# Cross-attention's first maxima ahead of the other batch's open sums, in VectorE's order of a decoder layer

## The reference

```python
x = x + attention(layernorm(x), Wq, bq, Wk, bk, Wv, bv, Wo)        # two corner scores set to -1e9
# cross-attention: the softmax runs over the heads, not over the keys
Q, K, V = split_heads(query @ Wq + bq), split_heads(ctx @ Wk + bk), split_heads(ctx @ Wv + bv)
energy = jnp.einsum('bhqd,bhkd->bhqk', Q, K) / sqrt(16)
energy = jnp.where(mask == 0, -1e10, energy)
attention = jax.nn.softmax(energy, axis=1)
x = x + jnp.einsum('bhqk,bhkd->bhqd', attention, V) merged @ Wo + bo
x = x + nvfp4_linear(silu(nvfp4_linear(ln(x), gate)) * nvfp4_linear(ln(x), up), down)
```

## Time and profile before

| | us |
|---|---|
| median of 3 runs (lowest, highest) | 573.68 (573.54, 574.16) |
| the profiled execution, its own time | 574.91 |
| its span in the profile | 573.2 |
| TensorE busy | 532.9 (93%) |
| VectorE busy | 503.2 (88%) |
| ScalarE busy | 344.8 (60%) |
| GpSimd busy | 343.8 (60%) |

### The profile page before, as it was taken

The page is one execution under the profiler, slowest core; times in us unless marked ns, Lnnn a source line. Parts: engine busy times, 40 slices in busy tenths (PEclk is TensorE's granted clock), DMA queues, the critical chain, the costliest instruction groups (busy, mean ns, idle before and its releaser), DMA issues. The chain is left out here.

```text
span 573.2 us, 14885 instructions
## 1 busy us (share of the span) xinstructions
PE 532.9 (93%) x6148; PEld 384.5 (67%) x6157; DVE 503.2 (88%) x674; ACT 344.8 (60%) x601; POOL 343.8 (60%) x262
## 2 busy tenths in 40 slices
PE   7899999999899999999999999999999887989787
PEld 6777777777567777777776777777777643534444
DVE  5887888798889888898899899899899989899987
ACT  3655766767554665467565765675568454766644
POOL 3111424323318776777897979867898885666750
PEclk9999999999999999999999999999999988989997
DMA  8910000000110011101110111011100000000001
GB/s 217 314 64 1 2 3 3 2 1 2 42 40 1 11 39 48 48 6 45 48 44 4 50 48 45 6 48 48 39 11 9 9 11 8 1 19 19 20 18 56
DMA packets 16645, 20.78 MB, mean 36 GB/s; under 512 B 2821, under 2 KB 14322, under 8 KB 16578
## 3 DMA queue, kind: packets, MB, share of 16 engines
q1 hardware_dynamic: 14800, 19.18, 11.2%
q10 hardware_dynamic: 1778, 0.66, 0.6%
HBM read 16.16 MB, written 1.84 MB: 31 GB/s over the span
## 5 line engine op out<-in xcount | busy, mean ns | idle before, releaser
L427 POOL TENSOR_TENSOR work<-work,rden 125x1792 f32<-125x1792 f32 x48 | 172.5, 3593 | 3.8
L1029 ACT ACTIVATE work<-scores 125x896 f32<-125x896 f32 x96 | 88.9, 985 | 95.4 <-PE scores L1458 95.4
L717 DVE TENSOR_REDUCE negmax<-scores 125x112 bf16<-125x1792 f32 x48 | 97.2, 2025 | 18.6 <-PE scores L1448 18.1
L725 DVE TENSOR_REDUCE den<-work 125x56 f32<-125x896 f32 x96 | 102.4, 1066 | 10.1 <-ACT work L1029 10.0
L425 POOL TENSOR_TENSOR rden<-rden,stays 125x112 f32<-125x112 f32 x48 | 22.2, 462 | 64.7 <-DVE rden L730 63.9
L1448 PE MATMUL scores<-qz,kT 32*125 32x224 f32 x768 | 50.5, 377 | 2.4 <-ACT work L1029 1.7
L1458 PE MATMUL scores<-negmax,identb 125*125 125x448 bf16 x192 | 45.1, 357 | 7.8 <-DVE negmax L717 7.6
L1484 PE MATMUL head_out<-work,v 125*32 125x112 f32 x1536 | 49.2, 268 | 0.0
L1555 PE MATMUL wide<-ctxT,ck 128*128 128x375 f32 x128 | 48.6, 500 | 0.0
L630 DVE TENSOR_REDUCE a_mpad<-scores 112x8 bf16<-112x896 f32 x32 | 33.5, 1092 | 15.2 <-PE scores L1350 15.1
L1569 PE MATMUL wide<-cv,ctxT 128*125 128x256 f32 x192 | 46.7, 379 | 0.0
(11 more groups left out here) (274 smaller groups left out, 1174.3 us busy)
## 6 DMA issues: line engine op xcount, KB each, us to landing
ctx_sb<-in_ctx SPq DMA_DIRECT2D x16, 375.0 KB
mask_sb<-in_mask_Bx1xSxS_if SPq DMA_DIRECT2D x16, 164.1 KB, 5.6
xsx<-in_x SPq DMA_DIRECT2D x4, 448.0 KB, 10.1
out_x<-ores SPq DMA_DIRECT2D x6, 256.0 KB, 2.2
a_raw_w<-in_L_ffn_gate_w SPq DMA_DIRECT2D x1, 1024.0 KB, 9.0
a_raw_w<-in_L_ffn_up_w SPq DMA_DIRECT2D x1, 1024.0 KB, 11.6
a_raw_w<-in_L_ffn_down_w SPq DMA_DIRECT2D x1, 1024.0 KB, 13.6
xt<-xsx SPq DMA_DIRECT2D x4, 112.0 KB, 2.2
```

Source lines behind the costliest of these rows:

```text
L427: pool.tensor_tensor(ex2[0:KP, kc], ex2[0:KP, kc], over, ALU.mult).then_inc(s["prob"], 1)
L717: dve.tensor_reduce(negmax[0:KP, :], scores[0:KP, :, 0:4 * TOK].rearrange("p j (h t) -> p t j h", h=4), AX.XY, ALU.max, negate=True).then_ ...
L725: link(dve.tensor_reduce(den[0:KP, kc, half], ex2[0:KP, kc, :, half, :].rearrange("p g t s -> p t g s"), AX.XY, ALU.add))
L1029: act.activation(ex2[0:KP, kc, 4 * i:4 * i + 4].rearrange("p (j m) t s -> p j m s t", m=NE), scores[0:KP, 2 * i:2 * i + 2, 0:4 * TOK].rear ...
```

## The change

In VectorE's loop over the turns of cross-attention, the maxima of (now, 0) are issued ahead of the first half sum of (old, 2) instead of behind it. The two instructions and all others stay as they are, and no wait is added or removed. In turn 0 there is no `old` and the order is the same.

```diff
                     third, fourth = early(n, 2), early(n, 3)
+                    if now:
+                        key_max(now, 0)
                     if old:
                         head_sum(old, 2, 0)
-                    if now:
-                        key_max(now, 0)
                     if n == 0:
                         outputs(B - 1)
```

## The result

| | before | after |
|---|---|---|
| median of 14 runs each, us | 573.92 (572.97 to 575.71) | 572.17 (570.44 to 573.13) |
| after / before, 95% interval | | 0.9963 (0.9952 to 0.9975) |
| profiled execution: span, us | 573.2 | 569.4 |
| its granted clock of TensorE, mean | 0.982 | 0.991 |
| start of the first maxima of turn 0 | 157.03 | 157.46 |

The kernel became 0.37% faster (0.25 to 0.48%): 573.92 x 0.0037 = 2.1 us; the two medians themselves are 1.75 us apart. The forecast was 571.9 and 1.8 us. The stretch from the first maxima of turn 0 to those of turn 15 was the same in the two profiled executions of either kernel, to 0.04 us, and most of what follows is read from it.

A forecast was written before the change was run, and what follows sets the result against it. TensorE bounds cross-attention's turns, VectorE counting only where TensorE waits for it. Gained 3.88 less 2.07 given back nets -1.81 us: from the 573.68 median to 571.9, a gain of 0.3%, range 570.4 to 574.0.

The forecast's parts named there:

- the eight latenesses: First maxima of turns 5, 7, 8, 9, 10, 12, 14, 15 start when scores are there: 3.88 us gained.
- turns in time: the second maxima don't move: Turns 2 to 6, 8, 10, 12, 13: idle pieces of 1.07 take up the half sum's 1.06, costing nothing.
- turns 7 and 9: Second maxima late, partly hidden before the exponentials, and third maxima late: 0.18 given back each, 0.36 together.
- turn 11 into 12: x_varp, tied to GpSimd's qz, holds VectorE 0.44 longer, delaying turn 12's first maxima: 0.42 given back, bounds 0.1 and 0.92.
- GpSimd in 6, 8, 10, 13: Product for the last third of keys comes 1.06 later, 1.03 hidden: 0.38 given back in all, bounds nothing and 4.24.
- turn 14: GpSimd's scale chain waits for VectorE's block maxima, 0.21 later, delaying its product and qz: 0.45 given back, bounds 0.18 and 1.06.
- turn 15, second maxima: No idle ahead of them, so 1.06 is paid, less 0.60 from a shorter instruction: 0.46 given back, bounds 0.46 and 1.06.
- 0.14 after the end of the scores is the earliest start: Read from turn 6: first maxima can start no sooner than 0.14 after scores end; lateness is counted from there.
- The late second maxima: In turns 7, 9, 11 and 14, one more instruction leaves 0.62 idle for 1.06: second maxima 0.44 late.
- The slower rival: GpSimd bounds turns 6, 8, 10, 13 if its 1.03 is not slack: 4.24 paid, net +2.05, 575.7 us; chance 0.10.
- The two holds: Instructions held by GpSimd's products shorten: turn 1's tiny one from 1.375 to under 0.5, turn 15's from 1.23 to 0.63.
- a rival for no change: Give-backs double (573.9 us) or TensorE's clock takes the gain, a slow stretch being worth near 1.5 (573.4); chance 0.22.

The follow-up runs named there:

- Run 5: The change made only in the late turns 5, 7, 8, 9, 10, 12, 14 and 15, against the kernel before; ratio 0.9954 (0.9935 to 0.9972).
- run 3: Order of the kernel before, but VectorE doesn't wait for the end of each first half sum, against the kernel before; ratio 0.9974 (0.9960 to 0.9989).
- run 8: The change plus no wait of VectorE for its own first half sums, against the kernel before; ratio 0.9928 (0.9902 to 0.9953).
- run 6: The change in all turns but 7, 9, 11, 14 and 15, against the kernel before; ratio 0.9951 (0.9935 to 0.9967).
- Run 10: The change in all turns but 15, against the kernel before; ratio 0.9942 (0.9923 to 0.9961).
- run 7: The change plus x_shifted moved behind the second maxima in its five turns, against the kernel before; ratio 1.0042 (1.0022 to 1.0062).

## Why the prediction was right

Point by point, in us of the loop, taken from turn lengths (end of the first scores to the next) in the profiles:

| step | forecast | measured |
|---|---|---|
| the eight latenesses gone | 3.88 | 3.88, but for turn 12 (below) |
| start 0.06 instead of 0.14 after the scores, 15 turns | none | 15 x 0.08 = 1.2 |
| turns in time: the second maxima don't move | 0 | 0 (0.13 to 0.14 behind their scores) |
| turns 7 and 9 | -0.36 | -0.28 - 0.27 |
| turn 11 into 12 | -0.42 | -0.22 - 0.27 |
| GpSimd in 6, 8, 10, 13 | -0.38 | about -0.05 |
| turn 14 | -0.45 | -0.54 |
| turn 15, second maxima | -0.46 | -0.53 |
| sum | 1.81 | 2.9; seen as a whole, 302.52 - 299.59 = 2.9 |

For the measured column the turn of before without its lateness and without the 0.08 is the base. Turn 7 was 19.07 - 0.22 - 0.08 = 18.77 long and became 19.05. Turn 14 was 19.14 - 0.23 - 0.08 = 18.83 and became 19.37.

**What bounds the kernel** was read rightly: TensorE sets the turn, and VectorE's lateness is TensorE's to the last tenth. Run 5 shows that the eight turns named by the rows hold the gain.

**The number is nearer than the account.** Forecast 1.8, measured 1.75 by the medians and 2.1 by the ratio: that closeness is in part luck. Up to the third maxima of turn 15 the change is worth 2.9 at an equal clock, 1.1 more than forecast. The medians show less because the changed kernel's executions had the lower clock more often, which no step of the prediction foresaw.

**The step that was mis-sized** is "0.14 after the end of the scores is the earliest start". That was read from turns in which a half sum with its own wait stood ahead of the maxima; run 3 shows that the wait made 0.08 of it. It is worth 1.2 in the change.

**The late second maxima** were 0.52 late in turns 7, 9 and 11, not 0.44, and the third ones of 7 and 9 0.21. The 0.44 was 1.06 - 0.62. From the first to the second maxima of turn 7 VectorE took 298.39 - 291.46 = 6.93 where it had taken 298.58 - 292.19 = 6.39, so 0.54 more: in its new place the half sum takes 1.12 up to the next instruction (293.40 to 294.52), and not 1.06, and the last half sum takes 1.11 up to the maxima (297.28 to 298.39), where the one before took 1.08 up to its idle time. In turn 15 it is 0.53 for the 0.46. Without VectorE's waits for its first half sums (run 8) the 6.93 is 6.68, so these waits have a share in it; which of the 0.10 is theirs no run shows.

**GpSimd** was late by 1.06 as worked out, and its product ended at the very moment at which TensorE wants it, but the 0.05 of a handover that I had put on top was already within the slack: 0.38 became 0.05. The slower rival rested on this place, and it is the nearest miss in the profile: slack of 0.05 to 0.11 where it was 1.01 to 1.03. In turn 14 it did happen, twice. TensorE waits 0.21 there for the product behind the scale chain, which I had 0.21 later, and 0.30 for the product of (13, 1), which I had not followed. The turn's 0.54 is near the forecast of 0.45 partly by luck, since its second maxima were only 0.16 late and not 0.4.

**The two holds** came out as worked out from the rows: 0.35 for the tiny instruction of turn 1 (under 0.5), 0.72 for x_varp, with 0.27 left at turn 12 above a start in time (0.42 forecast against a start at 0.14), and 0.63 for the one of turn 15.

**The clock** was a rival for no change. I priced one slow stretch at 1.5; the changed kernel with and without the one of turn 15 differs by 299.59 - 298.54 = 1.05. The clock moves single executions by more than the change does, both ways. Of the timed executions of the two kernels whose clock is listed, 26 of the changed one and 87 of the one before, those with an equal mean clock compare so (medians, number, all chips together): at 0.982, 575.06 (11) and 572.46 (7); at 0.985, 574.48 (22) and 571.50 (10); at 0.988, 573.29 (20) and 570.44 (3). That is 2.6 to 3.0, the 2.9 of the loop, so at an equal clock nothing of it is lost in the feed-forward part. At the three other clocks that both kernels had, with one to three executions of the changed one, it is 2.4 to 3.2. The comparisons of all executions show less, 2.1 and 2.6 us by the ratios, since those of the changed kernel had a lower clock more often: 6 of 26 were at 0.988 or above, of the kernel before 42 of 87. Why stays open. The longer stand in turn 15 (2.30 instead of 1.91) doesn't explain it: run 5, where TensorE stands 2.31 there, had 8 of 12 executions at 0.988 or above, and run 6, where it stands 1.90, had 3 of 12. Run 10, whose turn 15 is as before, had 0.985 in all six.

## What to carry to other kernels

Look for the instruction that stands between a late engine and the work that the bound engine waits for, and read each turn alone: here 8 turns of 16 held the whole gain, and the busy shares showed none of it. What is moved back lands in idle time only as long as there is some; list, turn by turn, the idle time behind the new place, for the engine itself and for each engine that it feeds. And a wait of an engine for its own last instruction is not free even where it is long satisfied: taken out where nothing reads the result yet, it gave 0.26% by itself in the old order (run 3), and 1.09 us of loop on top of the change (run 8).

## What the runs showed of the hardware

- A maxima instruction with one wait started 0.06 after the end of the matmuls it waits for; with a wait for VectorE's own last sum ahead of that, 0.13 or 0.14, in every turn from 1 to 14 in which VectorE was in time, in both orders and at idle times from 0.16 to 0.73. Without that wait it was 0.06 to 0.07 at an idle time of 0.65 too (run 3).
- A two-input instruction of VectorE that came while GpSimd was in a product of 3.6 stood until its end: 1.74 instead of 0.63, over 0.56 after the product's end (run 7). A tensor_scalar on 128x2 numbers did the same (0.72 instead of 0.17, ended 0.03 after GpSimd's). Half sums that lay wholly within such products took 1.03 to 1.08, the others 1.02 to 1.09.
- The kernel before had a median of 576.12 in executions with a mean granted clock of 0.979 (10 of them) and of 573.29 at 0.988 (20), while its loop up to turn 15 was equal to 0.04 in the two that were profiled. In both of these the clock fell in turn 15 and behind it, where TensorE stands for others, and not once ahead of it: the mean granted clock was 1.00 in every stretch read up to 445 us.
